# Attention output projection with its LayerNorms (stage A4): the PE order changed so that the next tile's projection is issued ahead of the current tile's transposes, and a second xn2_bf buffer

## The chip, the cores and the metric

The kernel runs on all 8 cores of one Trainium2 chip, the same program on each. Cores 0 to 3 are one die and cores 4 to 7 the other. The metric is the device time of the slowest core in microseconds (us). No core sends anything to another, so each core's time is that of its own program.

## The reference

One transformer layer with "sandwich" norms over x of 2 x 4096 x 2048, in float32:

```python
x = x + layernorm(attn(layernorm(x), wq, wk, wv, wo))
x = x + layernorm(ffn(layernorm(x), up_w, down_w, up_scale, down_scale, output_scale))
```

attn is 32 query heads over 8 key/value heads of 64, with rotary positions, a full softmax over 4096 keys, and the output projection by wo (2048 x 2048). ffn takes the signs of its weights (8192 x 2048 and 2048 x 8192), with a relu between. layernorm has no weight: (x - mean) / sqrt(var + 1e-5) over the 2048 features of a row. What the change touches is this part of it, for the 1024 rows of a core:

```python
a   = attn_heads @ wo              # 1024 x 2048
xr2 = x + layernorm(a)             # kept for the second residual
xn2 = layernorm(xr2)               # input of the ffn, wanted transposed
```

## The kernel before, in words

Each core has 1024 query rows of one of the two batch entries, in 8 tiles of 128 rows. Its input is rolled so that its own rows are rows 0 to 1023. It goes through six stages, one after the other, and between them full_barrier() makes every engine wait for all semaphores, all DMAs among them:

- A1 (L249 to L401): LayerNorm, transposes, keys and values for all 4096 rows, in 32 tiles. Its loop is already staggered by one tile.
- A2 (L413 to L488): queries of the own rows.
- A3 (L499 to L642): attention, 16 pairs of heads by 32 key chunks. Beside it the FFN's weights go through SBUF to bf16 scratch in HBM (scr_up, scr_dn).
- A4 (L653 to L752): the output projection, two LayerNorms, and the transposes into xn2T. This is the stage that the change is in.
- FFN (L757 to L861): four quarters of up and down projection. Panels of signs are loaded by transposing DMAs on SyncE's queue (L782, L819), signed on ScalarE (L788, L825), and multiplied in 4 groups of 32 matmuls (L800, L836).
- Final (L868 to L927): scale, transposes, the last LayerNorm, output.

The code writes each engine's program down by hand. p.do appends one instruction to one engine's list, p.wait appends a semaphore wait to it, and p.flush emits the lists. So the order of an engine's instructions is the order of the p.do calls for it, and an instruction behind a wait cannot overtake it. p.wait leaves out a wait that the engine has already made for the same or a later count.

A4 runs over the tiles tl = 0 to 7 (L681). All buffers that the stage has two of are picked by par = tl % 2: woPs (two PSUM tensors of 128 x 2048 f32, which together fill PSUM), xbufs, xr2t, and the statistics columns (sl = par * 8). xn2_bf and aps are single. For one tile, in the order of the code:

1. SyncE loads x (L688, by the helper load, so it shows at L145), after the residual add of tile tl-2 has freed xbufs[par].
2. TensorE does 64 matmuls of 128 x 512 into woP (L694), after wo_free[par]: the last copy of tile tl-2 out of the same woP.
3. layernorm_stats on woP (L700; its lines are L177 to L202): ScalarE squares and sums (L179), and with psum_in=True VectorE's sum (L184) waits for that, then three operations of one column on VectorE, then Ln and Exp on ScalarE (L197, L200). VectorE normalises into aps (L702) and adds x into xr2t (L706).
4. SyncE spills xr2t to HBM (L717, shown at L145 as xr2sp<-xr2t). This wait is ahead of the next tile's load in SyncE's queue.
5. layernorm_stats on xr2t (L719), then VectorE writes the normalised tile in bf16 to xn2_bf (L721).
6. Twice: TensorE does 8 transposes of 128 x 128, as matmuls with the identity, into the first 1024 columns of the same woP (L733), and VectorE copies them into xn2T (L738). The second half's transposes wait for the first half's copy (tp_gate).

The waits of step 6 stand in TensorE's list between the 64 matmuls of tile tl and those of tile tl+1.

Of the kernel before, what the change touches and what calls it, by code (L numbers as in the profile page):

```python
# [8 lines left out]
BF16 = mybir.dt.bfloat16  # L9
# [8 lines left out]
A4_STAGE = 3  # L18
# [69 lines left out]
def build_nc():  # L88
    nc = bass.Bass("TRN2", target_bir_lowering=False)
# [26 lines left out]
    with g:  # L116
        with nc.Block() as block:
            p = P(nc, block)
# [29 lines left out]
            def finish(src_fn):  # L148
                for tl in range(8):
# [27 lines left out]
            def layernorm_stats(ap_fn, sl, deps, stats_gate, psum_in=False):  # L177
                p.wait("scalar", *(list(deps) + [stats_gate]))
                t_ssq = p.do("scalar", lambda e: e.activation(  # L179
                    sqscr[:], ap_fn(), AF.Square, accum_out=stats[:, sl + 1:sl + 2]), sig="s")  # L180
                p.wait("vector", *(list(deps) + [stats_gate]))
                if psum_in:
                    p.wait("vector", t_ssq)
                t_sum = p.do("vector", lambda e: e.reduce_sum(  # L184
                    stats[:, sl:sl + 1], ap_fn(), axis=AX.X), sig="v")
                p.wait("vector", t_sum)
                t_mean = p.do("vector", lambda e: e.tensor_scalar(
                    stats[:, sl + 2:sl + 3], stats[:, sl:sl + 1], 1.0 / 2048, None, ALU.mult), sig="v")
# [13 lines left out]
                return t_var, t_rstd  # L202
# [301 lines left out]
            for i in range(64):  # L504
                par = i % 2
# [7 lines left out]
            for i in range(16):  # L513
                for hh in range(2):
                    par = (i * 2 + hh) % 2
# [137 lines left out]
            s4 = g.enter_context(ExitStack())  # L653
            wo_sb = s4.enter_context(nc.sbuf_tensor("wo_sb", [128, 16 * 2048], BF16, side="right"))
            xr2t = [s4.enter_context(nc.sbuf_tensor(f"xr2t{i}", [128, 2048], F32, side="right")) for i in range(2)]
            xn2_bf = s4.enter_context(nc.sbuf_tensor("xn2_bf", [128, 2048], BF16, side="right"))
            aps = s4.enter_context(nc.sbuf_tensor("aps", [128, 2048], F32, side="right"))
            xn2T = g.enter_context(ExitStack())
            xn2T_sb = xn2T.enter_context(nc.sbuf_tensor("xn2T", [128, 16 * 1024], BF16))
# [3 lines left out]
            woPs = [woP0, woP1]  # L663
# [10 lines left out]
            wo_free = [None, None]  # L674
            xb_free4 = [xb_free[0], xb_free[1]]
            stats_free4 = [stats_free[0], stats_free[1]]
            xr2_free = [None, None]
            xn2_free = None
            t_spill = [None] * 8
            t_x2ev = None  # L680
            for tl in range(8):  # L681
                par = tl % 2
                woP = woPs[par]
                xb = xbufs[par]
                xrt = xr2t[par]
                sl = par * 8
                p.wait("sync", xb_free4[par])
                t_x = load(lambda xb=xb: xb[:], lambda tl=tl: x[tl * 128:(tl + 1) * 128, :],  # L688
                           sig="lx%d" % par)
                p.wait("tensor", t_wo, t_aoT_ready, wo_free[par])  # L690
                t_mm = None
                for ic in range(16):
                    for s_ in range(4):
                        t_mm = p.do("tensor", lambda e, ic=ic, s_=s_, tl=tl, woP=woP: e.matmul(  # L694
                            woP[:, s_ * 512:(s_ + 1) * 512],
                            aoT[:, ic * 1024 + tl * 128: ic * 1024 + tl * 128 + 128],
                            wo_sb[:, ic * 2048 + s_ * 512: ic * 2048 + (s_ + 1) * 512],
                            start=(ic == 0), stop=(ic == 15)),
                            sig="t" if (ic == 15 and s_ == 3) else None)
                t_var, t_rstd = layernorm_stats(lambda woP=woP: woP[:], sl, (t_mm,), stats_free4[par], psum_in=True)  # L700
                p.wait("vector", t_rstd, t_var)
                t_ap = p.do("vector", lambda e, woP=woP, sl=sl: e.tensor_scalar(  # L702
                    aps[:], woP[:], stats[:, sl + 2:sl + 3], stats[:, sl + 6:sl + 7],
                    ALU.subtract, ALU.mult), sig="v")
                p.wait("vector", t_x, t_ap, xr2_free[par], t_spill[tl - 2] if tl >= 2 else None)
                t_xr2 = p.do("vector", lambda e, xrt=xrt, xb=xb: e.tensor_add(  # L706
                    xrt[:], aps[:], xb[:]), sig="v")
                xb_free4[par] = t_xr2
                if A4_STAGE == 2:
                    xb_free4[par] = t_xr2  # L710
                    stats_free4[par] = t_ap
                    xr2_free[par] = t_xr2
                    wo_free[par] = t_ap
                    t_spill[tl] = None
                    continue
                p.wait("sync", t_xr2)
                t_spill[tl] = load(lambda tl=tl: xr2sp[tl * 128:(tl + 1) * 128, :],  # L717
                                   lambda xrt=xrt: xrt[:], sig="sp%d" % par)
                t_var2, t_rstd2 = layernorm_stats(lambda xrt=xrt: xrt[:], sl, (t_xr2,), t_ap)  # L719
                p.wait("vector", t_rstd2, t_var2, xn2_free)  # L720
                t_xn2 = p.do("vector", lambda e, xrt=xrt, sl=sl: e.tensor_scalar(  # L721
                    xn2_bf[:], xrt[:], stats[:, sl + 2:sl + 3], stats[:, sl + 6:sl + 7],
                    ALU.subtract, ALU.mult), sig="v")
                stats_free4[par] = t_xn2
                xr2_free[par] = t_xn2
                t_tp_last = None
                tp_gate = t_ap
                for hb in range(2):
                    p.wait("tensor", t_xn2, tp_gate)
                    t_tp = None  # L730
                    for j in range(8):
                        ic = hb * 8 + j
                        t_tp = p.do("tensor", lambda e, ic=ic, j=j, woP=woP: e.matmul(  # L733
                            woP[:, j * 128:(j + 1) * 128], xn2_bf[:, ic * 128:(ic + 1) * 128],
                            id_bf[:], start=True, stop=True), sig="t" if j == 7 else None)
                    t_tp_last = t_tp
                    p.wait("vector", t_tp)
                    t_x2ev = p.do("vector", lambda e, hb=hb, tl=tl, woP=woP: e.tensor_copy(  # L738
                        bass.AP(xn2T_sb, (hb * 8) * 1024 + tl * 128,
                                [[16 * 1024, 128], [1024, 8], [1, 128]]),  # L740
                        woP[:, 0:1024].rearrange("p (i c) -> p i c", c=128)), sig="v")
                    tp_gate = t_x2ev
                xn2_free = t_tp_last
                wo_free[par] = t_x2ev

            dbg_dump("xr2", lambda: xr2t[1][:], p.barrier_tok("v"))
            dbg_dump("xn2T", lambda: xn2T_sb[:], p.barrier_tok("v"))
# [27 lines left out]
            for qt in range(4):  # L775
                t_hid = [None] * 16
                for pn in range(4):
                    par = pn % 2
# [13 lines left out]
                    for hcl in range(4):  # L792
# [4 lines left out]
                        for ic in range(16):  # L797
                            for s_ in range(2):
                                t_um = p.do("tensor", lambda e, ic=ic, s_=s_, apar=apar,
                                            par=par, hcl=hcl: e.matmul(  # L800
                                    accP[:, apar * 1024 + s_ * 512: apar * 1024 + (s_ + 1) * 512],
                                    pan[par][:, ic * 512 + hcl * 128: ic * 512 + hcl * 128 + 128],
                                    xn2T_sb[:, ic * 1024 + s_ * 512: ic * 1024 + (s_ + 1) * 512],
                                    start=(ic == 0), stop=(ic == 15)),
# [9 lines left out]
                for pn in range(4):  # L814
                    par = pn % 2
# [73 lines left out]
            for tl in range(8):  # L889
                par = tl % 2  # L890
                sl = par * 8
# [89 lines left out]
```

How the kernel before makes its waits and increments, by code:

```python
            def body(e, items=items):  # L75
                for it in items:
                    if it[0] == "op":
                        _, fn, sig, inc = it
                        ins = fn(e)
                        if sig is not None:
                            ins.then_inc(sems[sig], inc)
                    else:
                        _, sig, val = it
                        e.wait_ge(sems[sig], val)
```

## Time and profile before

| what | us |
|---|---|
| two runs, median | 3864.4 (3807.41 and 3921.38) |
| the profiled execution | 3807.01 |
| its span on the slowest core (core 2) | 3805.3 |
| spans of the 8 cores | 3792.0 to 3805.3 |
| PE busy in the span | 2739.0 (72%), x11256 |
| DVE busy | 1158.6 (30%) |
| ACT busy | 1441.0 (38%) |

The profile is of the slowest core in one execution. PE is TensorE's matmuls, PEld its weight loads (they overlap PE), DVE is VectorE, ACT ScalarE, POOL GpSimd, SP SyncE; a q behind a name is that engine's queue of DMA issues. A share of busy time is an average over stages that have different limits, so the stage of the change is read by itself. The 0.854 to 0.856 of granted TensorE clock that the eight cores have over the span is a mean too: the engine runs at 1.2 or at 2.4 GHz, and a PEclk of 1.00 for a stretch means 2.4 GHz all through it. In a timeline row, adjacent like instructions are joined (x62 is 62 of them), some matmul records are missing (so x62 and x63 stand for 64), and the bracket says how long the engine was idle before the row and what ended that.

### The profile page before, as it was taken

To read this page: it belongs to the slowest core of one execution; us is meant where nothing else is said; L and a number is where in the kernel's file an instruction comes from. 1 tells how busy PE (TensorE), PEld (TensorE's weight loads), DVE (VectorE), ACT (ScalarE), POOL (GpSimd) and SP (SyncE) were. 2 spreads that over 40 slices of the span, in tenths; PEclk is the share of its full clock that TensorE was granted. 3 is DMA by queue.
4 is the path that set the end of the run, shared out by engine and by line. 5 is a ranking of instruction groups with operands and counts; after the bars stand their busy time and mean duration, and the time that the engine had idled before them with its cause. 6 is when DMAs were issued, how large, how long until landed. Compare 5 with 4: busy or idle time off the path is not lost.

```text
span 3805.3 us, 30359 instructions; the slowest of 8 cores (3792.0 to 3805.3 us)
## 1 busy us (share of the span) xinstructions
PE 2739.0 (72%) x11256; PEld 1051.2 (28%) x11394; DVE 1158.6 (30%) x1324; ACT 1441.0 (38%) x1285; POOL 59.9 (2%) x108
## 2 busy tenths in 40 slices
PE   2555555467888888788888885354499999999962
PEld 1222222122222222222222221122244444444431
DVE  3555555374222222222222222234211111111135
ACT  1111110004777777777777774111222222222211
POOL 0000000000010000000000000000000000000000
PEclk8777777799898998988889987676799999999985
DMA  5111110413888899500000002311233333333313
GB/s 123 56 47 53 55 56 22 67 23 91 184 192 197 196 214 219 123 1 1 0 1 0 1 1 46 82 60 66 56 74 73 75 68 71 75 71 71 71 52 143
DMA packets 330851, 292.62 MB, mean 77 GB/s; under 512 B 283219, under 2 KB 295636, under 8 KB 314324
## 3 DMA queue, kind: packets, MB, share of 16 engines
q1 hardware_dynamic: 299988, 185.78, 16.8%
q0 software_dynamic: 28416, 88.12, 14.5%
q10 hardware_dynamic: 2304, 16.78, 1.3%
q8 instruction: 94, 1.54, 0.2%
q14 instruction: 49, 0.40, 0.0%
HBM read 227.71 MB, written 83.89 MB: 82 GB/s over the span
## 4 chain that ended last, share of the span: by engine, by line
PE 48%; DVE 17%; ACT 12%; issue 10%; SPq 8%; DMA 4%; another core or an unknown queue 2%; DVEq 0%; POOL 0%; ACTq 0%; POOLq 0%
PE accP L836 7%; PE pvA L586 7%; ACT expB L618 7%; PE scB L610 6%; PE accP L800 6%; PE scA L610 4%; SPq L782 4%; SPq L819 4%; PE vP L374 4%; PE pvB L586 3%; PE kP L369 3%; PE woP L694 3%; DVE stats L184 3%; DVE r_sb L638 3%; DMA wq_sb<-wq 2%
## 5 line engine op out<-in xcount | busy, mean ns | idle before, releaser
L618 ACT ACTIVATE expA<-scA,ebias 128x1024 bf16<-128x1024 f32 x512 | 570.5, 1114 | 350.5 <-PE scB L610 274.6
L618 ACT ACTIVATE expB<-scB,ebias 128x1024 bf16<-128x1024 f32 x512 | 567.0, 1107 | 0.6
L800 PE MATMUL accP<-xn2T,pan 128*128 128x512 bf16 x2006 | 447.6, 383 | 56.1 <-ACT pan L788 54.0
L836 PE MATMUL accP<-hid,pan 128*128 128x512 bf16 x2008 | 447.0, 382 | 23.8 <-ACT pan L825 21.4
L610 PE MATMUL scB<-QT,KT 64*128 64x512 bf16 x1024 | 313.1, 386 | 73.1 <-ACT expB L618 54.0
L633 DVE COPY pvs_sb<-pvA 65x1024 f32<-65x1024 f32 x16 | 19.5, 1221 | 1098.8 <-PE pvA L586 1098.8
L586 PE MATMUL pvA<-expA,VT 128*65 128x512 bf16 x1024 | 327.3, 402 | 0.0
L610 PE MATMUL scA<-QT,KT 64*128 64x512 bf16 x1024 | 321.0, 395 | 7.5 <-DVE QT L473 4.2
L586 PE MATMUL pvB<-expB,VT 128*65 128x512 bf16 x1024 | 313.5, 388 | 2.0 <-ACT expB L618 1.7
L800 PEld LDWEIGHTS accP<-xn2T,pan 128*128 128x128 bf16 x2048 | 201.1, 99 | 302.4 <-issue 67.0
L836 PEld LDWEIGHTS accP<-hid,pan 128*128 128x128 bf16 x2048 | 200.7, 98 | 270.1 <-issue 34.6
L825 ACT ACTIVATE pan<-pan 128x8192 bf16<-128x8192 bf16 x16 | 112.5, 7030 | 361.9 <-DMA pan<-scr_dn 361.9
L788 ACT ACTIVATE pan<-pan 128x8192 bf16<-128x8192 bf16 x16 | 112.5, 7030 | 333.7 <-DMA pan<-scr_up 333.7
L807 DVE TENSOR_SCALAR hid<-accP,ups_sb 128x1024 bf16<-128x1024 f32 x64 | 82.2, 1284 | 421.7 <-PE accP L800 421.7
L638 DVE RECIPROCAL r_sb<-pvs_sb 1x1024 f32<-1x1024 f32 x32 | 207.2, 6511 | 0.5
L341 PE MATMUL tpP<-id_bf,xn_bf 128*128 128x128 bf16 x512 | 62.4, 298 | 196.4 <-DVE xnT_kv L355 91.2
L437 PE MATMUL kP<-wq_sb,xnT_own 128*128 128x512 bf16 x499 | 121.7, 395 | 99.6 <-DMA wq_sb<-wq 67.1
L374 PE MATMUL vP<-wv_sb,xnT_kv 128*128 128x512 bf16 x384 | 168.5, 439 | 5.3 <-issue 5.3
L694 PE MATMUL woP<-wo_sb,aoT 128*128 128x512 bf16 x500 | 124.7, 412 | 60.1 <-DMA wo_sb<-wo 59.1
L369 PE MATMUL kP<-wk_sb,xnT_kv 128*128 128x512 bf16 x360 | 157.0, 436 | 0.0
L557 PE MATMUL pvA<-r_sb,ones_f 1*64 1x512 f32 x64 | 58.2, 1062 | 127.2 <-DVE r_sb L638 127.2
L849 DVE TENSOR_TENSOR dacc<-accP,dacc 128x1024 f32<-128x1024 f32 x48 | 58.8, 1225 | 295.7 <-PE accP L836 295.7
(85 smaller groups left out, 1938.2 us busy)
## 6 DMA issues: line engine op xcount, KB each, us to landing
f0b<-upw POOLq DMA_DIRECT2D x64, 512.0 KB, 6.9
scr_up<-f0b SPq DMA_DIRECT2D x64, 512.0 KB, 3.7
f0b<-dnw POOLq DMA_DIRECT2D x32, 1024.0 KB, 11.8
scr_dn<-f0b SPq DMA_DIRECT2D x32, 1024.0 KB, 7.2
xbuf<-x SPq DMA_DIRECT2D x24, 1024.0 KB, 5.8
xbuf<-x ACTq DMA_DIRECT2D x16, 1024.0 KB, 4.9
wq_sb<-wq POOLq DMA_DIRECT2D x4, 2048.0 KB, 18.2
wo_sb<-wo POOLq DMA_DIRECT2D x1, 8192.0 KB, 55.0
```

Of the source, the lines that this page charges most:

```text
L369: p.do("tensor", lambda e, ic=ic, par=par, xnT=xnT, colw=colw, colo=colo: e.matmul(kP[:, par * 512:(par + 1) * 512], xnT[:, ic * colw + co ...
L374: t_kv = p.do("tensor", lambda e, ic=ic, par=par, xnT=xnT, colw=colw, colo=colo: e.matmul(vP[:, par * 512:(par + 1) * 512], xnT[:, ic * co ...
L437: t_q = p.do("tensor", lambda e, ic=ic, tl=tl, tpar=tpar, qtr=qtr: e.matmul(kP[:, tpar * 512:(tpar + 1) * 512], xnT_own[:, ic * 1024 + tl ...
L586: t_pv = p.do("tensor", lambda e, kc=kc, s_=s_, hx=hx, g_=g_: e.matmul(pv[hx][0:65, s_ * 512:(s_ + 1) * 512], VT[:, kc * 520 + g_ * 65: kc ...
L610: rbase=rbase, pi=pi: e.matmul(sc[hx][:, s_ * 512:(s_ + 1) * 512], KT[rbase:rbase + 64, ptile * 4096 + kc * 128: ptile * 4096 + kc * 128 + ...
L618: t_exp[hx] = p.do("scalar", lambda e, hx=hx, kc=kc: e.activation(ex[hx][:, (kc % 2) * 1024:(kc % 2 + 1) * 1024], sc[hx][:], AF.Exp, bias= ...
L638: t_rs[hx] = p.do("vector", lambda e, hx=hx: e.reciprocal(r_sb[hx][:], pvs_sb[hx][64:65, 0:1024]), sig="v")
L694: t_mm = p.do("tensor", lambda e, ic=ic, s_=s_, tl=tl, woP=woP: e.matmul(woP[:, s_ * 512:(s_ + 1) * 512], aoT[:, ic * 1024 + tl * 128: ic ...
L782: t_pl = p.do("sync", lambda e, ic=ic, pn=pn, qt=qt, par=par: e.dma_start(out=pan[par][:, ic * 512:(ic + 1) * 512], in_=scr_up[qt * 2048 + ...
L800: par=par, hcl=hcl: e.matmul(accP[:, apar * 1024 + s_ * 512: apar * 1024 + (s_ + 1) * 512], pan[par][:, ic * 512 + hcl * 128: ic * 512 + h ...
L819: t_pl = p.do("sync", lambda e, j=j, pn=pn, qt=qt, par=par: e.dma_start(out=pan[par][:, j * 512:(j + 1) * 512], in_=scr_dn[pn * 512:(pn + ...
L836: par=par, dcl=dcl: e.matmul(accP[:, apar * 1024 + s_ * 512: apar * 1024 + (s_ + 1) * 512], pan[par][:, j * 512 + dcl * 128: j * 512 + dcl ...
```

## The change

The body of the loop is split into three functions: a4_mm (load of x and the 64 matmuls), a4_ln (both LayerNorms, the spill, xn2_bf) and a4_tp (transposes and copies). The driver calls them staggered. xn2_bf becomes a pair, with xn2_free kept for each. Nothing else in the stage changes: waits, shapes and counts of instructions stay, and A4_STAGE's branch, which was not taken, is gone.

```diff
-            xn2_bf = s4.enter_context(nc.sbuf_tensor("xn2_bf", [128, 2048], BF16, side="right"))
+            xn2_bf = [s4.enter_context(nc.sbuf_tensor(f"xn2_bf{i}", [128, 2048], BF16, side="right"))
+                      for i in range(2)]
...
-            for tl in range(8):
+            def a4_mm(tl):
...
                 p.wait("sync", xb_free4[par])
...
+                return t_mm, t_x
+
+            def a4_ln(tl, t_mm, t_x):
...
-                p.wait("vector", t_rstd2, t_var2, xn2_free)
-                t_xn2 = p.do("vector", lambda e, xrt=xrt, sl=sl: e.tensor_scalar(
-                    xn2_bf[:], xrt[:], stats[:, sl + 2:sl + 3], stats[:, sl + 6:sl + 7],
+                xnb = xn2_bf[par]
+                p.wait("vector", t_rstd2, t_var2, xn2_free[par])
+                t_xn2 = p.do("vector", lambda e, xrt=xrt, sl=sl, xnb=xnb: e.tensor_scalar(
+                    xnb[:], xrt[:], stats[:, sl + 2:sl + 3], stats[:, sl + 6:sl + 7],
                     ALU.subtract, ALU.mult), sig="v")
...
+                xn2s[tl] = (t_xn2, t_ap)
+
+            def a4_tp(tl):
...
+                wo_free[par] = t_ev
+                return t_ev
+
+            xn2_free = [None, None]
+            mmres = [None] * 8
+            for i in range(9):
+                if i < 8:
+                    mmres[i] = a4_mm(i)
+                if i - 1 >= 0:
+                    t_x2ev = a4_tp(i - 1)
+                if i < 8:
+                    a4_ln(i, *mmres[i])
```

TensorE at the start of A4, after the attention's last matmuls (L557): before, 64 matmuls of the projection (woP from wo_sb and aoT) and 16 transposes (woP from id_bf and xn_bf, which is the name given to xn2_bf).

```order
L557 MATMUL pvB<-r_sb,ones_f 64x512 x2
L85 UNCONDITIONAL_BRANCH
L694 MATMUL woP<-wo_sb,aoT 128x512 x64
L733 MATMUL woP<-id_bf,xn_bf 128x128 x16
L694 MATMUL woP<-wo_sb,aoT 128x512 x64
```

The same place now; L694 has become L695 and L733 L746.

```order
L557 MATMUL pvB<-r_sb,ones_f 64x512 x2
L85 UNCONDITIONAL_BRANCH
L695 MATMUL woP<-wo_sb,aoT 128x512 x128
L746 MATMUL woP<-id_bf,xn_bf 128x128 x16
L695 MATMUL woP<-wo_sb,aoT 128x512 x64
```

The matmuls of tile 1 have moved ahead of the transposes of tile 0, and so on through the stage.

TensorE at the end of A4, where the FFN (accP) begins: before, each tile's transposes follow its own matmuls.

```order
L694 MATMUL woP<-wo_sb,aoT 128x512 x64
L733 MATMUL woP<-id_bf,xn_bf 128x128 x16
L85 UNCONDITIONAL_BRANCH
L800 MATMUL accP<-xn2T,pan 128x512 x512
L836 MATMUL accP<-hid,pan 128x512 x512
```

The same place now.

```order
L695 MATMUL woP<-wo_sb,aoT 128x512 x64
L746 MATMUL woP<-id_bf,xn_bf 128x128 x32
L85 UNCONDITIONAL_BRANCH
L824 MATMUL accP<-xn2T,pan 128x512 x512
L860 MATMUL accP<-hid,pan 128x512 x512
```

The transposes of tiles 6 and 7 now stand behind tile 7's matmuls. VectorE's order through a tile and into the next is as it was; only the line numbers differ (now):

```order
L184 TENSOR_REDUCE stats<-woP 128x1
L187 TENSOR_SCALAR stats<-stats 128x1
L190 TENSOR_TENSOR stats<-stats 128x1
L193 SCALAR_TENSOR_TENSOR stats<-stats 128x1
L712 TENSOR_SCALAR aps<-woP,stats 128x2048
L717 TENSOR_TENSOR xr2t<-aps,xbuf 128x2048
L184 TENSOR_REDUCE stats<-xr2t 128x1
L187 TENSOR_SCALAR stats<-stats 128x1
L190 TENSOR_TENSOR stats<-stats 128x1
L193 SCALAR_TENSOR_TENSOR stats<-stats 128x1
L726 TENSOR_SCALAR xn_bf<-xr2t,stats 128x2048
L751 CAST xn2T<-woP 128x8x128 x2
```

The next tile's L184 follows the two copies, before and now. ScalarE's order in the stage and SyncE's (load, spill, load, spill) have not moved either.

## Rows read from the trace of the kernel before

**Rows 1.** the page: costliest groups, the stage's output projection; the columns stand in the text
```profile
L694 PE MATMUL woP<-wo_sb,aoT 128*128 128x512 bf16 x500 | 124.7, 412 | 60.1 <-DMA wo_sb<-wo 59.1
```

**Rows 2.** timeline of all engines, tiles 0 and 1: start us, us, engine line op, idle before
```profile
2407.74 15.18 PE L694 MATMUL woP<-wo_sb,aoT 128*128 128x512 bf16 x62 [59.06 <-DMA wo_sb<-wo]
...
2426.37 2.29 DVE L184 TENSOR_REDUCE stats<-woP 128x1 f32<-128x2048 f32 x1 [75.03 <-ACT sqscr L179]
...
2432.82 2.29 DVE L706 TENSOR_TENSOR xr2t<-aps,xbuf 128x2048 f32<-128x2048 f32 x1
...
2435.57 0.43 SPq L145 DMA_DIRECT2D xbuf<-x  x1
...
2439.22 1.35 DVE L721 TENSOR_SCALAR xn_bf<-xr2t,stats 128x2048 bf16<-128x2048 f32 x1 [0.86 <-ACT stats L200]
...
2440.71 1.01 PE L733 MATMUL woP<-id_bf,xn_bf 128*128 128x128 bf16 x8 [17.79 <-DVE xn_bf L721]
2441.83 1.23 DVE L738 CAST xn2T<-woP 128x1024 bf16<-128x1024 f32 x1 [1.26 <-PE woP L733]
...
2443.20 1.01 PE L733 MATMUL woP<-id_bf,xn_bf 128*128 128x128 bf16 x8 [1.48 <-DVE xn2T L738]
...
2444.01 16.03 PE L694 MATMUL woP<-wo_sb,aoT 128*128 128x512 bf16 x63
2444.32 1.22 DVE L738 CAST xn2T<-woP 128x1024 bf16<-128x1024 f32 x1 [1.26 <-PE woP L733]
...
2460.14 1.88 ACT L179 ACTIVATE sqscr<-woP 128x2048 f32<-128x2048 f32 x1 [21.09 <-PE woP L694]
...
2462.21 2.29 DVE L184 TENSOR_REDUCE stats<-woP 128x1 f32<-128x2048 f32 x1 [16.66 <-ACT sqscr L179]
```

**Rows 3.** timeline of all engines, the stage's last copy and the next stage's start
```profile
2694.96 1.23 DVE L738 CAST xn2T<-woP 128x1024 bf16<-128x1024 f32 x1 [1.26 <-PE woP L733]
2696.57 33.82 SPq L782 DMA_TRANSPOSE pan<-scr_up  x26
```

**Rows 4.** waits of 2400 to 2700 us: who waited for whom, us in total, times, longest
```profile
ACT sqscr L179 <- PE woP L694: 146.6, 7, 21.6
PE woP L733 <- DVE xn_bf L721: 134.1, 8, 17.8
```

**Rows 5.** timeline of PE, later tiles of the stage
```profile
2514.91 16.41 PE L694 MATMUL woP<-wo_sb,aoT 128*128 128x512 bf16 x63
...
2691.36 1.01 PE L733 MATMUL woP<-id_bf,xn_bf 128*128 128x128 bf16 x8 [16.77 <-DVE xn_bf L721]
```

**Rows 6.** granted clock by stretch: length, busy time (x count) of five engines, PEclk, DMA
```profile
core 2: us, PE busy (x) PEld busy (x) DVE busy (x) ACT busy (x) POOL busy (x), PEclk, DMA share, GB/s
2444.00:2461.00 17.00, 15.99 (x66) 6.68 (x64) 1.22 (x1) 0.86 (x1) 0.00 (x0) 0.88 0.00 1
2474.00:2510.00 36.00, 16.73 (x78) 8.08 (x80) 14.18 (x14) 5.46 (x10) 0.00 (x0) 0.74 0.19 65
2697.00:2790.00 93.00, 58.03 (x257) 26.11 (x264) 10.27 (x8) 22.37 (x4) 0.00 (x0) 0.81 0.33 72
2840.00:2960.00 120.00, 114.04 (x520) 51.52 (x530) 19.65 (x16) 30.64 (x5) 0.00 (x0) 1.00 0.33 71
3612.00:3616.00 4.00, 4.00 (x10) 1.50 (x12) 0.00 (x0) 0.00 (x0) 0.00 (x0) 0.57 0.67 79
```

**Rows 7.** timeline of PE, two panels of the feed-forward stage
```profile
3611.99 29.47 PE L836 MATMUL accP<-hid,pan 128*128 128x512 bf16 x125 [2.06 <-ACT pan L825]
3641.64 27.79 PE L836 MATMUL accP<-hid,pan 128*128 128x512 bf16 x126 [0.17 <-issue]
```

**Rows 8.** timeline of PE, the projection of the queries
```profile
775.68 3.61 PE L437 MATMUL kP<-wq_sb,xnT_own 128*128 128x512 bf16 x16 [1.25 <-DVE kq_bf L241]
```

**Rows 9.** DMA of the stage, issues: count, KB each, median us to landing
```profile
xr2sp<-xr2t SPq DMA_DIRECT2D x8, 1024.0 KB, 4.8
xbuf<-x SPq DMA_DIRECT2D x7, 1024.0 KB, 6.9
```

More of the change, by code:

```diff
@@ L680, in build_nc @@
             t_x2ev = None
-            for tl in range(8):
+            xn2s = [None] * 8
+            def a4_mm(tl):
                 par = tl % 2
@@ L684, in build_nc @@
                 xb = xbufs[par]
-                xrt = xr2t[par]
-                sl = par * 8
                 p.wait("sync", xb_free4[par])
@@ L699, in build_nc @@
                             sig="t" if (ic == 15 and s_ == 3) else None)
-                t_var, t_rstd = layernorm_stats(lambda woP=woP: woP[:], sl, (t_mm,), stats_free4[par], psum_in=True)
+                return t_mm, t_x
+            def a4_ln(tl, t_mm, t_x):
+                par = tl % 2
+                woP = woPs[par]
+                xb = xbufs[par]
+                xrt = xr2t[par]
+                sl = par * 8
+                t_var, t_rstd = layernorm_stats(lambda woP=woP: woP[:], sl, (t_mm,),
+                                                stats_free4[par], psum_in=True)
                 p.wait("vector", t_rstd, t_var)
@@ L704, in build_nc @@
                     ALU.subtract, ALU.mult), sig="v")
-                p.wait("vector", t_x, t_ap, xr2_free[par], t_spill[tl - 2] if tl >= 2 else None)
+                p.wait("vector", t_x, t_ap, xr2_free[par],
+                       t_spill[tl - 2] if tl >= 2 else None)
                 t_xr2 = p.do("vector", lambda e, xrt=xrt, xb=xb: e.tensor_add(
@@ L708, in build_nc @@
                 xb_free4[par] = t_xr2
[L709 to L715, printed above, removed]
                 p.wait("sync", t_xr2)
@@ L725, in build_nc @@
                 xr2_free[par] = t_xn2
+                xn2s[tl] = (t_xn2, t_ap)
+            def a4_tp(tl):
+                par = tl % 2
+                woP = woPs[par]
+                xnb = xn2_bf[par]
+                t_xn2, t_ap = xn2s[tl]
                 t_tp_last = None
                 tp_gate = t_ap
+                t_ev = None
                 for hb in range(2):
@@ L732, in build_nc @@
                         ic = hb * 8 + j
-                        t_tp = p.do("tensor", lambda e, ic=ic, j=j, woP=woP: e.matmul(
-                            woP[:, j * 128:(j + 1) * 128], xn2_bf[:, ic * 128:(ic + 1) * 128],
+                        t_tp = p.do("tensor", lambda e, ic=ic, j=j, woP=woP, xnb=xnb: e.matmul(
+                            woP[:, j * 128:(j + 1) * 128], xnb[:, ic * 128:(ic + 1) * 128],
                             id_bf[:], start=True, stop=True), sig="t" if j == 7 else None)
@@ L737, in build_nc @@
                     p.wait("vector", t_tp)
-                    t_x2ev = p.do("vector", lambda e, hb=hb, tl=tl, woP=woP: e.tensor_copy(
+                    t_ev = p.do("vector", lambda e, hb=hb, tl=tl, woP=woP: e.tensor_copy(
                         bass.AP(xn2T_sb, (hb * 8) * 1024 + tl * 128,
@@ L741, in build_nc @@
                         woP[:, 0:1024].rearrange("p (i c) -> p i c", c=128)), sig="v")
-                    tp_gate = t_x2ev
-                xn2_free = t_tp_last
-                wo_free[par] = t_x2ev
+                    tp_gate = t_ev
+                xn2_free[par] = t_tp_last
+                wo_free[par] = t_ev
[9 more added lines that the diff above has]
+                    a4_ln(i, *mmres[i])
             dbg_dump("xr2", lambda: xr2t[1][:], p.barrier_tok("v"))
```

## The prediction

> **What bounds the kernel now.** I read the page first, then the timeline of the stage that the change is in, then its waits, then the granted clock by stretch. On the page the output projection has 124.7 us of busy matmuls and one long wait, for wo_sb at its start [rows 1]. The stage runs from its first matmul at 2407.74 us [rows 2] to the end of its last copy, 2694.96 + 1.23 = 2696.19 us [rows 3]: 288.5 us. So PE is busy less than half of it. The waits say why, and they say it of two sides: ScalarE's squares waited for the projection 146.6 us in 7 times, and the transposes waited for xn2_bf 134.1 us in 8 times [rows 4]. Two engines that wait for one another by turns, each for about half the stage, do one job in series. The sum of the two is 280.7 us, nearly the whole stage.
>
> The timeline of tile 0 shows the series in detail [rows 2]. Matmuls from 2407.74 on. VectorE's sum over woP starts at 2426.37, the residual add at 2432.82, and xn2_bf is done at 2439.22 + 1.35 = 2440.57. Transposes start at 2440.71, and the second copy ends at 2444.32 + 1.22 = 2445.54. I call these the LayerNorm chain (2426.37 to 2440.57, 14.2 us) and the transposing tail (2440.71 to 2445.54, 4.83 us; with its handoff of 0.14, 4.97 us). Tile 1's matmuls start at 2444.01, in the tail, because the second half's transposes had been issued, and its square starts at 2460.14. From tile 0's transposes to tile 7's it is 2691.36 - 2440.71 = 250.65 us [rows 2, 5], which is 35.8 us per tile over 7.
>
> What stands behind the stage: the first panel load of the FFN is issued at 2696.57 us, 0.38 us after the last copy [rows 3]. The barrier lets nothing of the FFN start sooner. So A4 lies on the path that sets the end with its full length, and each us taken out of it should move everything behind it forward by one.
>
> **The change, part by part.** No instruction is added or removed, save that xn2_bf has two buffers. TensorE's list alone is reordered: 64 matmuls of tile i+1 now stand ahead of the transposes of tile i. What a tile then costs follows from who waits for whom:
>
> - The matmuls of tile i+1 write the woP that tile i-1 used, so they start at the end of tile i-1's second copy. On VectorE, the very next thing behind this copy is the sum of tile i's LayerNorm chain. So matmuls(i+1) and chain(i) start together and run beside each other.
> - The transposes of tile i need both to have ended: xn2_bf(i) by its data, matmuls(i+1) because they stand ahead in TensorE's list. Then comes the tail, and the next period starts.
>
> One period is therefore max(chain, matmuls) + tail. The square of tile i+1 (1.88 us, [rows 2]) is done on ScalarE during the tail, and the 2.07 us between square and sum that were on the path (2460.14 to 2462.21) are not on it any more.
>
> The chain is 14.2 us + 0.14 for the handoff. Does it stretch with PE working beside it? A copy of 1024 columns out of PSUM took 1.23 us with PE idle (2441.83) and 1.22 us with matmuls running (2444.32) [rows 2], so I take no stretch. The matmuls depend on the clock. At 2.4 GHz a panel of 128 of them took 27.79 us [rows 7], which gives 64 of them 13.9 us. In this stage they start at the lower level: a tile's 64 took 16.03 us in tile 1 [rows 2] and 16.41 in tile 3 [rows 5], with a granted clock of 0.88 over the stretch [rows 6], after an idle time of 17.79 us.
>
> Now PE will not be idle for 17 us. It will have only the tail: two bursts of 8 transposes with pauses of about 1.5 us for the copies, in 4.8 us. What the clock does after such a pause the stage doesn't show. Two rows are near. After 2.06 us of idleness an FFN panel of 128 took 29.47 us against 27.79 [rows 7], with a clock of 0.57 in its first 4 us [rows 6]: one fall, worth 1.7 us. After 1.25 us of idleness, 16 matmuls of the query projection took 3.61 us [rows 8], 0.22 each: no fall. The tail has 1.5 us at a time but three times over, so I take the fall: 13.9 + 1.7 = 15.6 us for the 64. The bounds are 13.9 (no fall) and 16.4 (as now).
>
> So matmuls (15.6) are longer than the chain (14.3), and the period is 15.6 + 4.8 = 20.4 us. Its bounds: without a fall the chain decides, 14.2 + 4.97 = 19.2; and as the 8 transposes of a burst would then also be at 2.4 GHz instead of 1.2, both bursts together save perhaps 0.8 us (128 columns at each level: 27.79 / 128 / 4 = 0.054 us against 0.107, 16 times), so 18.4. With matmuls as now, 16.4 + 4.8 = 21.2.
>
> The sum for the stage: up to the end of tile 0's tail nothing changes, 2445.54 - 2407.74 = 37.8 us; matmuls of tile 1 fit in the 17.6 us of tile 0's norms. Then 6 periods with matmuls of tiles 2 to 7 in them: 6 x 20.4 = 122.4. Then tile 7's chain and tail with nothing beside them: 19.2. Together 179.4 against 288.5 us: 109.1 less. With the bounds: 6 x 18.4 + 37.8 + 18.4 = 166.6 (121.9 less) and 6 x 21.2 + 37.8 + 19.2 = 184.2 (104.3 less).
>
> Edits that cost nothing here. The second xn2_bf lets xn2_bf(i) be written while transposes(i-1) could still read the first; in VectorE's order the copies of i-1 stand ahead anyway, so by itself it buys about nothing and costs nothing. The load of x(i+1) is issued as before, behind the spill of tile i in SyncE's queue, right after the residual add (2435.57 after 2432.82 + 2.29) [rows 2]. It lands 6.9 us later [rows 9], and the next residual add comes one period later, about 20 us instead of 36. It is covered with some 11 us to spare. What is late next in the stage is PE again, by the clock; VectorE is 1.2 us behind it.
>
> The sum is made against the profiled execution, 3807.01 us, which is the lower of the two kinds of run shown (3807.41 and 3921.38); their median is 57 us above it. 3807.0 - 109.1 = 3697.9, say 3698 us.
>
> On the clock there is a rule that speaks against so large a gain. Where all cores run dense matmuls the rows show 1.00: 520 recorded matmuls in 120 us [rows 6]. The Trainium skill, "TensorE: Matmul & The Clock Gate", section "Part 1: The HAM clock gate", holds that with three or more cores of a die in dense matmuls the whole die drops to 13/16 of 2.4 GHz and that one should budget 1.95 GHz. By that rule 64 matmuls would take 17.1 us, a period 21.9 and the stage 188, some 100 us less than before. This trace disagrees with the rule at the denser place, so the sum goes by 2.4 GHz.
>
> **The rivals.**
>
> *The chain decides.* The clock stays up through the tail, as after 1.25 us [rows 8], and the period is 18.4 to 19.2 us. For it: the pauses are shorter than 2.06 us, and 64 matmuls stand close around each. Against: three pauses in a row, with 1 us of work between. Time: 37.8 + 7 x 19.2 = 172.2, so 116 less, 3691 us; at 18.4, 3685.
>
> *The clock is as low as now.* 16.4 us for the matmuls, 3807.0 - 104.3 = 3703 us. For it: the tail's 4.8 us have under 2 us of PE work. Against: the idle time now is 17.79 us.
>
> *The overlap is taken back by x.* If the load for the next tile took not 6.9 us but 25, beside the spill, each residual add would wait for it; add to add is then 25 + 2.3 us for the add, 27.3 us per tile, and the stage gains 7 x (35.8 - 27.3) = 59.5 us: 3747 us, within 2%. It decides from a landing time of about 18 us on. Against: 6.9 us and 4.8 us [rows 9] at a DMA share of 0.19 in the stage [rows 6]; a period of 20 us doubles that share to under 0.4.
>
> *Slower.* The stage gets shorter, and the FFN pays for it by clock: TensorE comes out of A4 after denser work on all cores at once, and the FFN's 4096 matmuls (889 us at 27.79 / 128) are granted less than the 1.00 that they have now. At 0.81, which the stretch at the FFN's start has today [rows 6], they would take 208 us more: 3698 + 208 = 3906 us. It decides from a clock of 889 / (889 + 109) = 0.89 on. For it: one of the two runs shown is 114 us above the other, so something of this size exists. Against: the FFN's first panel is only loaded once A4 has ended [rows 3], so PE pauses between the stages, and inside the FFN the clock holds 1.00 at full density, so what A4 did before should not matter.
>
> **How the numbers follow.** Forecast (one fall per tile) 0.50; the chain decides 0.22; clock as now 0.18; x comes late, or something else takes back most of the overlap, 0.06; FFN at a lower clock 0.04. A measurement of this kernel can tell about 2% from no change, 76 us. The first three are all 104 us or more: faster 0.90, same 0.06, slower 0.04. The likeliest is 3698. Its own range is 3685 to 3703. The range I give reaches up to 3760: it takes in the late x (3747), and a median over runs such as the two shown, which lay 57 us above the profiled execution (3698 + 57 = 3755). Downward, 3680 leaves 5 us below the lowest bound, since the other parts of the kernel vary by a few us.
>
> **What would show it.** In the profile after: in the stage's timeline the 64 matmuls start within 0.2 us of VectorE's sum over the other woP; the period between tiles' transposes is 20.4 us (18.4 to 21.2) instead of 35.8; the transposes wait for the matmuls and hardly for xn2_bf (134.1 us before, under 20 after); ScalarE's squares wait for the projection in tile 0 but hardly later; from first matmul to last copy it is 179 us. The granted clock in a stretch of 64 matmuls tells the forecast (near 0.9, about 8 slow matmuls) from the chain rival (1.00). The FFN and the final stage keep their lengths. It is wrong if the period is above 25 us, if the residual add waits for the load of x, or if the FFN grows by over 20 us.

## The result, and the profile after

The changed kernel takes 3718.45 us, the median of 11 runs (3689.24 to 3823.93), against 3811.7 us of the kernel before (10 runs). In some runs of either kernel a whole die was held at a lower clock, which raises both medians, so the comparison is the ratio of the runs without that: 0.9708, interval 0.9681 to 0.9734. On 3807 us this is 111 us less (101 to 121). Forecast were 109 us less and 3698 us.

The profiled execution's span on its slowest core (core 4) is 3711.0 us. Its timeline shows two successive periods of the stage, a long one and a short one. The columns are as in [rows 2]; L695 is L694 of before, L746 is L733, L751 is L738, L726 is L721.

```profile
2464.65 0.61 PE L746 MATMUL woP<-id_bf,xn_bf 128*128 128x128 bf16 x8
...
2468.82 15.66 PE L695 MATMUL woP<-wo_sb,aoT 128*128 128x512 bf16 x63 [1.48 <-DVE xn2T L751]
2484.32 0.61 PE L746 MATMUL woP<-id_bf,xn_bf 128*128 128x128 bf16 x8
...
2486.41 0.61 PE L746 MATMUL woP<-id_bf,xn_bf 128*128 128x128 bf16 x8 [1.48 <-DVE xn2T L751]
...
2488.26 2.28 DVE L184 TENSOR_REDUCE stats<-woP 128x1 f32<-128x2048 f32 x1
2488.70 13.76 PE L695 MATMUL woP<-wo_sb,aoT 128*128 128x512 bf16 x62 [1.69 <-DVE xn2T L751]
...
2494.77 2.29 DVE L717 TENSOR_TENSOR xr2t<-aps,xbuf 128x2048 f32<-128x2048 f32 x1 [0.17 <-DVE aps L712]
...
2501.16 1.35 DVE L726 TENSOR_SCALAR xn_bf<-xr2t,stats 128x2048 bf16<-128x2048 f32 x1 [0.86 <-ACT stats L200]
2502.56 1.88 ACT L179 ACTIVATE sqscr<-woP 128x2048 f32<-128x2048 f32 x1 [1.57 <-PE woP L695]
2502.66 0.61 PE L746 MATMUL woP<-id_bf,xn_bf 128*128 128x128 bf16 x8 [0.19 <-DVE xn_bf L726]
2503.37 1.22 DVE L751 CAST xn2T<-woP 128x1024 bf16<-128x1024 f32 x1 [0.86 <-PE woP L746]
```

The matmuls are recorded from 0.44 us after the start of VectorE's sum over the other woP (2488.70 after 2488.26). The first of them is probably a missing record, since the idle time before the row is 1.69 us where it is 1.48 elsewhere, so the true distance is nearer 0.2 us. The two run side by side, where in [rows 2] the sum waited for them. In the first period the 64 matmuls go from 2468.82 to the transposes at 2484.32, 15.5 us, and the transposes follow without a wait: here TensorE is the longer path. In the second they take 13.76 us as recorded, and the transposes wait 0.19 us for xn2_bf: here the LayerNorm chain is, 2488.26 to 2502.51, 14.25 us, which is what it took with nothing beside it. From transposes to transposes it is 19.67 us in the first (2464.65 to 2484.32) and 18.34 us in the second.

The granted clock of the two stretches tells them apart (0.89 and 1.00), and the third row is the whole stage. Columns as in [rows 6].

```profile
2469.00:2484.00 15.00, 14.95 (x62) 6.50 (x62) 11.15 (x11) 3.00 (x6) 0.00 (x0) 0.89 0.41 124
2489.00:2502.00 13.00, 12.95 (x61) 5.88 (x61) 10.31 (x11) 3.00 (x6) 0.00 (x0) 1.00 0.33 88
2411.00:2583.00 172.00, 128.41 (x628) 60.13 (x640) 110.82 (x104) 40.90 (x65) 0.00 (x0) 0.89 0.31 92
```

The whole stage of the kernel before, on core 2, for comparison:

```profile
2408.00:2696.00 288.00, 139.81 (x628) 65.54 (x637) 111.97 (x104) 41.01 (x65) 0.00 (x0) 0.72 0.15 55
```

The same numbers of recorded matmuls (628), VectorE (104) and ScalarE (65) instructions are done in 172 us instead of 288. VectorE and ScalarE are busy as long as before; TensorE needs 11 us less for the same matmuls, because it is granted 0.89 of the clock where it was 0.72. PE's busy share of the stage has gone from about half to three quarters. The waits of the stage, as in [rows 4]:

```profile
PE woP L746 <- DVE xn_bf L726: 20.0, 4, 15.6
ACT sqscr L179 <- PE woP L695: 15.8, 6, 3.3
PE woP L746 <- DVE xn2T L751: 12.2, 8, 1.8
```

The two waits that together filled the stage, 134.1 and 146.6 us, are 20.0 and 15.8. Of the 20.0 us, 15.6 is one wait: tile 7's transposes, which have no next tile's matmuls ahead of them. The end of the stage:

```profile
2578.48 1.01 PE L746 MATMUL woP<-id_bf,xn_bf 128*128 128x128 bf16 x8 [15.64 <-DVE xn_bf L726]
...
2582.44 1.23 DVE L751 CAST xn2T<-woP 128x1024 bf16<-128x1024 f32 x1 [1.26 <-PE woP L746]
2584.05 36.42 SPq L806 DMA_TRANSPOSE pan<-scr_up  x28
...
2617.64 2.76 PE L824 MATMUL accP<-xn2T,pan 128*128 128x512 bf16 x6 [35.30 <-ACT pan L812]
```

As in [rows 3], the FFN's first load is issued 0.4 us after the last copy, so the FFN moved forward with the end of the stage.

Averaged over the eight cores, first matmul of the stage to last burst of transposes fell from 287.3 to 171.7 us, 115.6 less. The slowest core's span fell by less, 3805.3 - 3711.0 = 94.3 us. The stage isn't where this difference went. The profiled execution took 3712.5 us, and five other runs of the same kernel took 3689.2 to 3698.0. On core 4 the stage began 4.1 us later than on core 2 before (2411.82 against 2407.74), most of it a longer wait for wo (62.35 against 59.06 us), and the FFN (first matmul to last) took 957 us against 941. The page says as what. First the two FFN groups of before, then those of after:

```profile
L800 PE MATMUL accP<-xn2T,pan 128*128 128x512 bf16 x2006 | 447.6, 383 | 56.1 <-ACT pan L788 54.0
...
L836 PE MATMUL accP<-hid,pan 128*128 128x512 bf16 x2008 | 447.0, 382 | 23.8 <-ACT pan L825 21.4
```

```profile
L824 PE MATMUL accP<-xn2T,pan 128*128 128x512 bf16 x2006 | 451.0, 385 | 62.7 <-ACT pan L812 60.4
L860 PE MATMUL accP<-hid,pan 128*128 128x512 bf16 x2008 | 449.9, 384 | 29.5 <-ACT pan L849 27.1
```

Idle time before the matmuls is 12.3 us longer, nearly all of it the wait for signed panels, and 6.3 us are in the matmuls. But the FFN varies so much without any change to it: by core 930 to 944 us in the execution of before, 933 to 957 in this one. Whether the change has a part in it needs more executions; they are below.

### The profile page after: what moved, and what is told of

The parts are those of the page before. It is cut to its first block, busy times and chain, and to the rows that moved or that the text cites. A ratio compares the mean times of both kernels' runs of the same rounds, so it can differ in the third digit from the quotient of the medians.

```text
span 3711.0 us, 30358 instructions; the slowest of 8 cores (3666.3 to 3711.0 us)
## 1 busy us (share of the span) xinstructions
PE 2731.6 (74%) x11256; PEld 1047.0 (28%) x11394; DVE 1157.7 (31%) x1324; ACT 1441.3 (39%) x1285; POOL 59.8 (2%) x108
## 3 DMA queue, kind: packets, MB, share of 16 engines
q1 hardware_dynamic: 299988, 185.78, 18.3%
## 4 chain that ended last, share of the span: by engine, by line
PE 48%; DVE 16%; ACT 11%; issue 10%; SPq 8%; DMA 5%; another core or an unknown queue 2%; DVEq 0%; POOL 0%; ACTq 0%; POOLq 0%
PE pvA L586 7%; PE accP L824 7%; ACT expB L618 7%; PE scB L610 6%; PE accP L860 6%; PE scA L610 4%; SPq L806 4%; SPq L843 4%; PE vP L374 4%; PE pvB L586 4%; PE kP L369 3%; DVE r_sb L638 3%; DVE stats L184 3%; PE woP L695 2%; DMA wq_sb<-wq 2%
## 5 line engine op out<-in xcount | busy, mean ns | idle before, releaser
L695 PE MATMUL woP<-wo_sb,aoT 128*128 128x512 bf16 x500 | 118.1, 397 | 72.3 <-DMA wo_sb<-wo 62.4
L197 ACT ACTIVATE stats<-stats,epsb 128x1 f32<-128x1 f32 x56 | 16.5, 294 | 361.1 <-DVE stats L193 361.1
```

## The experiments

Each kernel is a small edit, of the changed kernel unless said otherwise; in the diffs, "..." marks lines left out. A ratio is to the kernel before, run in the same sitting; e4, e6 and e7 have none (e6 and e7 were run once). Besides, each is read by two stretches that other stages do not disturb, as means over the eight cores of the profiled execution: S, from the start of the first projection matmul to that of the last transpose, and B, up to the FFN's first matmul, which takes in the load of wo, the stage and the first panel. B is counted from the start of the attention's last matmul into pvA (L557); that is 6.4 us ahead of its very last one, into pvB, in every run, so differences of B do not depend on it. Where an expectation says "the attention's last matmul", it is this one. Before: S 287.3, B 387.2 us. Changed: S 171.7, B 273.0.

**The second buffer alone** (e1_buffer_only).

```diff
-            for i in range(9):
-                if i < 8:
-                    mmres[i] = a4_mm(i)
-                if i - 1 >= 0:
-                    t_x2ev = a4_tp(i - 1)
-                if i < 8:
-                    a4_ln(i, *mmres[i])
+            for i in range(8):
+                mmres[i] = a4_mm(i)
+                a4_ln(i, *mmres[i])
+                t_x2ev = a4_tp(i)
```

> The changed kernel with the pair of xn2_bf kept and the loop put back to matmuls, norms, transposes of one tile after the other. My theory (the order on TensorE does all of it): the stage is back at about 287 us from first matmul to last transpose, the time within 0.3% of the kernel before. Rival (the second buffer takes part of the gain): the stage is under 280 us and the time over 0.3% below before.

Measured: S 287.7, B 387.1 us; ratio 0.9974 (0.9951 to 0.9997). The stage is the one of before. Its timeline of PE:

```profile
2404.62 15.95 PE L695 MATMUL woP<-wo_sb,aoT 128*128 128x512 bf16 x64 [59.41 <-DMA wo_sb<-wo]
2438.36 1.01 PE L746 MATMUL woP<-id_bf,xn_bf 128*128 128x128 bf16 x8 [17.79 <-DVE xn_bf L726]
...
2441.65 16.23 PE L695 MATMUL woP<-wo_sb,aoT 128*128 128x512 bf16 x64
2474.39 1.01 PE L746 MATMUL woP<-id_bf,xn_bf 128*128 128x128 bf16 x8 [16.51 <-DVE xn_bf L726]
```

The period is back to 2474.39 - 2438.36 = 36.0 us, with the waits of 17.79 and 16.51 us of old. The ratio's interval ends just below 1; the stage shows no gain to go with it.

**The order alone** (e2_order_only): one xn2_bf, one xn2_free, the staggered driver kept.

```diff
-                      for i in range(2)]
+                      for i in range(1)]
...
-                xnb = xn2_bf[par]
-                p.wait("vector", t_rstd2, t_var2, xn2_free[par])
+                xnb = xn2_bf[0]
+                p.wait("vector", t_rstd2, t_var2, xn2_free[0])
...
-                xn2_free[par] = t_tp_last
+                xn2_free[0] = t_tp_last
```

> The changed kernel's order with a single xn2_bf. My theory: VectorE has the copies of tile i ahead of the write of xn2_bf for tile i+1 anyway, so the stage keeps its 171 to 173 us and the time its 0.971 of before. Rival (the pair is needed): the write waits for the transposes on a longer path, periods over 19.2 us, stage over 176 us.

Measured: S 171.4, B 271.2 us; ratio 0.9689 (0.9667 to 0.9711). All of the gain is there without the second buffer.

**Matmuls in the pauses of the tail** (e3_fill_pauses).

```diff
                     t_tp_last = t_tp
+                    for _ in range(5 if tl < 7 else 0):
+                        p.do("tensor", lambda e, woP=woP: e.matmul(
+                            woP[:, 1536:2048], id_bf[:], wo_sb[:, 0:512],
+                            start=True, stop=True))
```

> The changed kernel with 5 matmuls of 128x512 behind each burst of transposes (not for tile 7), whose result nobody reads, so that TensorE works in the pauses for the copies. My theory (every other tile pays 1.5 to 1.9 us for a clock that falls because of the pauses): the granted clock is 1.00 in all stretches of 64 matmuls, all periods are 18.3 us, and the stage is about 6 us shorter, 166 us. Rival (the LayerNorm chain would decide those tiles too, or the extra matmuls stand in the way): the stage is 171 us or more.

Measured: S 166.7, B 266.9 us; ratio 0.9678 (0.9654 to 0.9703). Timeline of PE on its slowest core:

```profile
2453.01 13.97 PE L695 MATMUL woP<-wo_sb,aoT 128*128 128x512 bf16 x62 [0.40 <-DVE xn2T L755]
2467.18 0.61 PE L746 MATMUL woP<-id_bf,xn_bf 128*128 128x128 bf16 x8 [0.20 <-DVE xn_bf L726]
...
2471.34 13.97 PE L695 MATMUL woP<-wo_sb,aoT 128*128 128x512 bf16 x63 [0.40 <-DVE xn2T L755]
2485.51 0.61 PE L746 MATMUL woP<-id_bf,xn_bf 128*128 128x128 bf16 x8 [0.20 <-DVE xn_bf L726]
```

The granted clock in its stretches of matmuls:

```profile
2435.00:2448.00 13.00, 12.95 (x61) 5.87 (x60) 10.37 (x11) 3.00 (x6) 0.00 (x0) 1.00 0.31 100
2453.00:2466.00 13.00, 12.89 (x59) 5.91 (x62) 10.30 (x11) 3.00 (x6) 0.00 (x0) 1.00 0.29 89
2471.00:2485.00 14.00, 13.60 (x63) 6.19 (x64) 11.31 (x12) 3.00 (x6) 0.00 (x0) 1.00 0.30 102
```

With pauses of 0.40 instead of 1.48 us the clock no longer falls. From the second of the six periods on, the matmuls take 13.97 us, the period is 18.33 us (2485.51 - 2467.18) and the transposes wait 0.20 us for xn2_bf, on this core in each. TensorE does 10 matmuls more per tile and the stage is 5 us shorter, as expected. So the long periods of the changed kernel were long by the clock, and the clock fell because of the pauses. In the total time the 5 us don't stand out from the spread of the runs.

**No gate on the second half's transposes** (e4_second_half_ungated).

```diff
...
-                            woP[:, j * 128:(j + 1) * 128], xnb[:, ic * 128:(ic + 1) * 128],
+                            woP[:, hb * 1024 + j * 128: hb * 1024 + (j + 1) * 128], xnb[:, ic * 128:(ic + 1) * 128],
...
-                        woP[:, 0:1024].rearrange("p (i c) -> p i c", c=128)), sig="v")
-                    tp_gate = t_ev
+                        woP[:, hb * 1024:(hb + 1) * 1024].rearrange("p (i c) -> p i c", c=128)), sig="v")
```

> The changed kernel with the second half's transposes written to columns 1024 to 2047 of woP, without waiting for the first half's copy. My theory (the tail is in every period in full): the two copies follow one another at once, the tail shrinks from 4.2 to 3.3 us in all 8 tiles, and the stage to about 164 us, a little less if the shorter pause also spares falls of the clock. Rival (tail hidden, matmuls alone decide): the stage stays at 171 us.

Measured: B 261.2 us, 12 less than the changed kernel and 10.0 less than e2, which has the changed order and was run beside it. (S is 160.6, but it ends at the last transpose, which here comes ahead of both copies, so B is the measure.) A ratio came only from the later run e11_ungated_again. Timeline of PE, where the 16 transposes are now one burst:

```profile
2482.26 1.05 PE L746 MATMUL woP<-id_bf,xn_bf 128*128 128x128 bf16 x16 [0.20 <-DVE xn_bf L726]
2485.48 13.97 PE L695 MATMUL woP<-wo_sb,aoT 128*128 128x512 bf16 x64 [2.16 <-DVE xn2T L751]
2499.64 1.05 PE L746 MATMUL woP<-id_bf,xn_bf 128*128 128x128 bf16 x16 [0.20 <-DVE xn_bf L726]
```

The tail is 3.22 us (2482.26 to 2485.48) instead of 4.2, and the period 17.38. Eight tails give the 8 us that were expected; the rest goes with falls of the clock that no longer come. On every core but one, a single one of the last five stretches of matmuls had a slow start (15.66 us here), and on that one none had, though the one pause left is 2.16 us, longer than either of the 1.48 it replaces.

**A longer chain** (e6_longer_chain).

```diff
                 p.wait("vector", t_rstd2, t_var2, xn2_free[par])
+                p.do("vector", lambda e, xrt=xrt, sl=sl: e.reduce_sum(
+                    stats[:, sl:sl + 1], xrt[:], axis=AX.X), sig="v")
```

> The changed kernel with one more sum over xr2t (2.29 us, 2.4 with its handoff) on VectorE ahead of the write of xn2_bf; its result is used by nobody. Theory A (chain and matmuls are level, and which is longer depends on the clock): all six periods become chain bound at 18.3 + 2.4 = 20.7 us, tiles 0 and 7 take 2.4 more each, so the stage is 172 + 6 x 1.5 + 4.8 = 186 us. Theory B (the matmuls decide in all six): only tiles 0 and 7 pay, 177 us. Theory C (the chain decides in all): 8 x 2.4 = 19 more, 191 us.

Measured: S 184.2 us, 12.5 more than the changed kernel; B 283.8. Theory A said 186, B 177, C 191, so A is nearest. Its waits on the slowest core for xn2_bf:

```profile
PE woP L748 <- DVE xn_bf L728: 29.2, 7, 18.0
```

Seven of the eight tiles now wait for xn2_bf, where it was four. With the chain at 16.6 us even matmuls with a slow start (15.66) are covered; the one tile that doesn't wait on this core is tile 1, whose transposes stand behind tile 2's matmuls, and these start after the longer idle time of tile 0.

**Fewer matmuls** (e7_fewer_matmuls).

```diff
-                for ic in range(16):
+                for ic in range(14):
...
-                            start=(ic == 0), stop=(ic == 15)),
-                            sig="t" if (ic == 15 and s_ == 3) else None)
+                            start=(ic == 0), stop=(ic == 13)),
+                            sig="t" if (ic == 13 and s_ == 3) else None)
```

> The changed kernel with 56 of the 64 matmuls of each tile: it leaves out the last 256 of the 2048 inner features of the product with wo. Theory A: matmuls fall to 12.1 us (13.8 with a fall of the clock) and are below the chain in every period, so a fall of the clock costs nothing, all periods are 18.3 us, and the stage from first matmul to last transpose is 6 us shorter plus 1.7 us of tile 0: 164 us. Theory B (matmuls decide in all six): 7 x 1.7 = 12 us less, 160 us. Theory C (the chain decides in all six): only tile 0's 1.7 us, 170 us.

Measured: S 166.0 us; A said 164, B 160, C 170, so A is nearest here too, but less clearly. An eighth less work for TensorE gave 5.7 us, of which 1.7 are tile 0's; leaving out 1.7 us in each period gave 4 us over six. Two starts of 56 matmuls, from its timeline of PE:

```profile
2468.04 13.78 PE L695 MATMUL woP<-wo_sb,aoT 128*128 128x512 bf16 x56 [1.48 <-DVE xn2T L751]
2482.22 0.61 PE L746 MATMUL woP<-id_bf,xn_bf 128*128 128x128 bf16 x8 [0.39 <-DVE xn_bf L726]
...
2486.39 14.84 PE L695 MATMUL woP<-wo_sb,aoT 128*128 128x512 bf16 x56 [1.48 <-DVE xn2T L751]
2501.06 0.61 PE L746 MATMUL woP<-id_bf,xn_bf 128*128 128x128 bf16 x8
```

And their granted clock, columns as in [rows 6]:

```profile
2468.10:2482.10 14.00, 13.72 (x56) 5.66 (x56) 11.28 (x11) 3.18 (x7) 0.00 (x0) 0.89 0.35 97
2486.40:2501.00 14.60, 14.60 (x56) 6.05 (x57) 11.32 (x11) 3.00 (x6) 0.00 (x0) 0.82 0.37 99
```

13.78 us (clock 0.89) is under the chain; 14.84 (clock 0.82) is just over it. I had counted 13.8 for all, so A's 164 was 2 us short: with less work between the pauses the clock fell in every stretch of matmuls on this core, and in some for longer than before. On every core three of the six periods were decided by the chain and three by TensorE. It is the same reading as e6 from the other side: the chain sets a floor of 18.3 us per period, and TensorE is over the floor only where the clock is low at its start.

**The load of wo in four** (e8_ungated_split_wo, e10_split_wo_rounds: one kernel, run twice), on top of the ungated version.

```diff
-            t_wo = load(lambda: wo_sb[:].rearrange("p (i c) -> p i c", c=2048),
-                        lambda: wo.ap().rearrange("(i p) c -> p i c", p=128),
-                        eng="gpsimd", sig="co")
+            t_wos = []
+            for qd, sg in enumerate(("co", "cw", "cq", "cu0")):
+                t_wos.append(load(
+                    lambda qd=qd: wo_sb[:, qd * 8192:(qd + 1) * 8192].rearrange(
+                        "p (i c) -> p i c", c=2048),
+                    lambda qd=qd: wo.ap().rearrange("(i p) c -> p i c", p=128)[
+                        :, qd * 4:(qd + 1) * 4, :],
+                    eng="gpsimd", sig=sg))
...
                 for ic in range(16):
+                    if ic % 4 == 0:
+                        p.wait("tensor", t_wos[ic // 4])
```

> The ungated version with the load of wo cut in four loads by inner feature, with a semaphore each, and each quarter of tile 0's matmuls waiting only for its own. If the wait for wo (59 us with one load) ends in full only at the last piece, three quarters of tile 0's matmuls move beside the load: the end of tile 0's matmuls comes some 7 to 8 us sooner after the attention stage, and the whole time falls by as much against the ungated version, to about 3670 us where the changed kernel has 3692. Rival: four loads take longer than one, and nothing is gained.

> The ungated version with the load of wo in four, again, in more rounds: from the attention's last matmul to the FFN's first the first run had 249 us on average over the cores, against 273 in the changed kernel and 387 before. If the rest of the kernel keeps its length, the time is 138 us below before: 0.964. Rival: part of it is given back in the FFN, 0.967 or more.

> The ungated version alone, again, in more rounds: 261 us from the attention's last matmul to the FFN's first, 126 below before, so 0.967 of before; between the changed kernel and the version with the load cut in four.

> The changed kernel as it is, on the same chip as the three others, to compare with them: 0.971 of before, stage 171 to 173 us, FFN 930 to 957 us by core as in the kernel before (my theory: the FFN is not touched; the rival of a slower clock in the FFN would show 945 us or more on all cores).

> The changed kernel on the same chip as the two: 271 to 273 us from the attention's last matmul to the FFN's first, 0.970 of before. If the differences in this stretch (12 and 24 us) reach the end, the three ratios are apart by 0.003 and 0.006 in this order.

These five belong together, three kernels in two sittings:

| kernel | B, us | FFN, us | ratio to before (interval) |
|---|---|---|---|
| changed, e9 | 270.8 | 941.9 | 0.9679 (0.966 to 0.9698) |
| changed, e12 | 270.2 | 935.8 | 0.968 (0.9644 to 0.9717) |
| ungated, e11 | 259.0 | 931.8 | 0.9653 (0.9623 to 0.9682) |
| ungated and wo in four, e8 | 249.1 | not compared | 0.9656 (0.9606 to 0.9707) |
| ungated and wo in four, e10 | 248.9 | 934.4 | 0.9646 (0.9609 to 0.9683) |

Ahead of these runs the changed kernel was expected at 271 to 273 us and 0.970, the ungated one at 261 and 0.967; both came out 1 to 2 us and 0.002 lower. The stretch B falls by 11 us without the gate (10.0 in e4 against e2) and by another 10 with the load in four (7 to 8 were expected). S does not compare for the last two, since there tile 0's matmuls begin under the load. The changed kernel run again has S 171.1 and 171.5 us, and by core an FFN of 933 to 950 (e9) and 929 to 946 (e12). In e10's timeline the matmuls of tile 0 start under the load:

```profile
2369.00 5.33 PE L703 MATMUL woP<-wo_sb,aoT 128*128 128x512 bf16 x15 [20.49 <-DMA wo_sb<-wo]
2381.36 6.16 PE L703 MATMUL woP<-wo_sb,aoT 128*128 128x512 bf16 x16 [7.02 <-DMA wo_sb<-wo]
2393.51 5.22 PE L703 MATMUL woP<-wo_sb,aoT 128*128 128x512 bf16 x16 [6.00 <-DMA wo_sb<-wo]
2405.43 1.01 PE L703 MATMUL woP<-wo_sb,aoT 128*128 128x512 bf16 x2 [6.70 <-DMA wo_sb<-wo]
```

The four loads together take no longer than the one: the last of tile 0's waits for wo ends 57.4 us after the end of the attention's last matmul in e10, and the one wait of e11 58.5 us after it (means over the cores), so the rival of a slower load falls. e10's own rival, that part of the gain is given back in the FFN, would show at 0.967 or more. The interval does not exclude that, but e10's FFN, 934.4 us, is no longer than the others'. In the total the ratios stand in the expected order, 0.968, 0.965, 0.965, but their intervals overlap: that the two further edits shorten the stretch by 21 us is shown, that the whole time follows to the last us is not.

## Why the prediction was right

**The series and what the reorder does to it.** Right as put. A period is the longer of chain and matmuls, plus the tail. e1 and e2 show that the order on TensorE does all of it and the second buffer none, as the forecast had costed it.

**The stage's sum: 179.4 us forecast, 171.9 measured** (core 4, 2411.82 to 2583.67). By its terms:

- Up to the end of tile 0's tail: 37.8 forecast, 37.6 measured (2411.82 to the matmuls at 2449.41).
- Tile 7 by itself: 19.2 forecast, 19.6 measured (2564.09, its sum, to 2583.67).
- Six periods: 6 x 20.4 = 122.4 forecast, 114.7 measured, 19.1 each. All of the miss is here, and it has two parts. The tail was taken at 4.8 us, the length it had with TensorE at 1.2 GHz; with the transposes right behind the matmuls it is at 2.4 GHz (a burst is 0.61 us instead of 1.01), and the tail is 4.2 us. I had put this into the lower bound only, and tied it to the absence of any fall. And a fall of 1.7 us was taken for every tile; it came in four of the six, and in the other two the chain's 14.25 us decided. So the first rival, "the chain decides", is true of two periods in six. The count is the same on 31 of the 32 cores of the four profiled executions with the changed order and its pauses (the changed kernel, e2, e9, e12); on the remaining one it is three and three.

The fall's own size, 1.7 us, was right where it came: 15.66 us for the 64 against 13.97 with the pauses filled (e3).

**What stands behind the stage.** The forecast said the rest keeps its length. FFN, mean over cores: 937.4 and 939.6 us in the two executions with the old order; 943.4, 941.9, 935.8 with the changed kernel, and 936.3, 940.1, 940.8, 938.4, 939.4, 934.4 and 931.8 in other experiments with the new order. The mean is 938.5 of the two and 938.2 of the ten. The rival of an FFN at a lower clock needed 109 us more to cancel the gain, and 945 us on all cores was the mark set ahead of e9; it falls. The 957 us of core 4 in the first profile is at the edge of what the FFN does by core; it came once more, 958 us on core 4 of e3. That the new order costs the FFN a us or two on average is neither shown nor excluded by these numbers.

**The late x.** Its landing time did grow, from 6.9 us [rows 9] to 8.9 (columns as there):

```profile
xr2sp<-xr2t SPq DMA_DIRECT2D x8, 1024.0 KB, 6.1
xbuf<-x SPq DMA_DIRECT2D x7, 1024.0 KB, 8.9
```

With 19 us between two residual adds it stays covered, and in the first timeline above the add (L717) waits only for aps, by 0.17 us.

**The total.** 109 us forecast, 111 (101 to 121) measured. The stage alone, with 116 us, is inside this interval as well. That the total came within 2 us is partly luck: the sum for the stage was 7 us off, and the total is not known to 7 us. The changed kernel's two other ratios, 0.9679 and 0.968, are 122 us less each. The median of 3718 us lies above 3698 for the reason given with the result, which is what the upper part of the range was for.

## What to carry to other kernels

When two engines' waits for one another add up to the length of a stage, look at the order in one engine's queue first: a step that waits (here 16 small transposes) holds back independent work that stands behind it, and moving that work ahead gained 3% without a single instruction or byte less. The new period is then a maximum, so it has to be worked out for both sides with the clock that each will have after the change, not the one it has today: here the two sides were level within 1.3 us, and e3, e6 and e7 each moved the balance by 1.7 to 2.4 us. A second buffer is worth asking about but not worth assuming: VectorE, which writes xn2_bf, had by its own order already waited for the transposes that read it.

## What was not expected of the hardware

TensorE's clock fell after pauses of 1.48 us, but only in four of six tiles of an otherwise equal sequence, mostly by turns (0.89 against 1.00 of granted clock in the second fence above), with pauses of 0.40 us in none, and with one pause of 2.16 us in place of two shorter ones in one of the last five on 15 of 16 cores (e4 and e11). The length of one pause alone does not tell. What does decide it stays open. And VectorE's chain of PSUM and SBUF work was as long with TensorE writing the other half of PSUM (14.25 us) as without (14.20): overlapping the two cost neither of them anything that the profile shows.
